# Normalising, elu parts and half of the expert scalings on ACT and POOL, and another opening, in a two-layer decoder kernel

## The reference

```python
x = _layernorm(x + _L0_attn_ref(x, ...))    # causal, 16 heads of 8; q and k normalised first
x = _layernorm(x + _L0_xattn_ref(x, ctx_1024, ctx_1024, ...))   # 16 heads, context of 154
x = _layernorm(x + _L0_ffn_ref(x, ...))     # 8 experts
x = _layernorm(x + _L1_attn_ref(x, ...))    # linear attention, phi = elu + 1
x = _layernorm(x + _L1_xattn_ref(x, ctx_1024, ...))   # 8 heads of 128, context of 154
x = _layernorm(x + _L1_ffn_ref(x, ...))     # silu(gate) * up, then down

def _layernorm(x, axis=-1, eps=1e-05):
    return (x - mean(x)) / sqrt(var(x) + eps)
# the experts
out = out + weights[:, e:e + 1] * (x @ expert_w[e] + expert_b[e])
# the linear attention
def phi(x): return jax.nn.elu(x) + 1.0
```

## Time and profile before

| | |
|---|---|
| runs | 677.26, 679.23, 681.54 us; median 679.23 |
| profiled execution | 679.57 us, span 677.8 us |
| busy | PE 526.4, DVE 443.4, ACT 294.6, POOL 144.3 us |
| granted TensorE clock, mean | 0.883 |

### The profile page before, as it was taken

One profiled execution on the slowest core, in us unless ns is written; L12 is line 12 of the kernel. 1 busy time (PEld: TensorE's weight loads), 2 busy tenths in 40 slices (PEclk: granted clock), 3 DMA queues, 4 the chain that ended last, 5 costly groups with the idle time before them and its releaser, 6 DMA issues. The chain is left out here.

```text
span 677.8 us, 12412 instructions
## 1 busy us (share of the span) xinstructions
PE 526.4 (78%) x4432; PEld 344.1 (51%) x4432; DVE 443.4 (65%) x1318; ACT 294.6 (43%) x713; POOL 144.3 (21%) x232
## 2 busy tenths in 40 slices
PE   3557798777898777887879779788897777878765
PEld 1434465433454354455755354565645464755653
DVE  3458777866788876745776988445887548456224
ACT  2333665554473243663542455753433352315631
POOL 8340002500010511222020102411202131214321
PEclk8675999977998878799978999887998989869888
DMA  7321100231200030010000000200000000000000
GB/s 197 114 82 49 49 3 24 62 87 31 55 3 2 16 81 2 16 48 2 2 18 1 3 2 10 55 2 0 18 2 1 1 1 0 1 0 16 2 0 15
DMA packets 27200, 18.19 MB, mean 27 GB/s; under 512 B 8333, under 2 KB 26885, under 8 KB 27013
## 3 DMA queue, kind: packets, MB, share of 16 engines
q1 hardware_dynamic: 22101, 13.14, 7.5%
q10 hardware_dynamic: 5040, 4.27, 2.1%
HBM read 5.58 MB, written 1.05 MB: 10 GB/s over the span
## 5 line engine op out<-in xcount | busy, mean ns | idle before, releaser
L1608 ACT ACTIVATE EX<-psum 128x1024 f32<-128x1024 f32 (+1 forms) x128 | 117.7, 975 | 54.5 <-PE psum L1209 38.7
L1809 DVE TENSOR_REDUCE nmax<-psum 128x2 f32<-128x768 f32 (+1 forms) x96 | 76.9, 862 | 20.4 <-PE psum L1182 20.1
L1176 PE MATMUL psum<-K,Q 48*128 48x154 bf16 (+4 forms) x512 | 55.9, 286 | 27.8 <-DMA K<-parts 6.9
L1804 DVE TENSOR_REDUCE nmax<-psum 128x4 f32<-128x616 f32 (+1 forms) x80 | 67.7, 876 | 8.0 <-PE psum L1176 6.5
L1203 PE MATMUL psum<-Q,K 51*128 51x512 bf16 (+3 forms) x320 | 50.2, 344 | 11.6 <-ACT EX L1608 4.2
L2073 DVE TENSOR_REDUCE nxmax<-psum 128x2 f32<-128x308 f32 x64 | 29.3, 473 | 38.3 <-PE psum L1441 37.0
L1089 POOL TENSOR_TENSOR GP<-REST,xrs 128x512 f32<-128x512 f32 (+1 forms) x48 | 32.8, 711 | 89.9 <-PE psum L1126 60.3
L1519 ACT COPY pvraw<-psum 128x512 f32<-128x512 f32 x32 | 18.7, 586 | 74.4 <-PE psum L1235 45.3
L1043 POOL TENSOR_SCALAR rstd_rest<-moments_rest 128x2 f32<-128x2 f32 x32 | 7.4, 231 | 199.5 <-DVE moments_rest L1852 199.4
L1176 PEld LDWEIGHTS psum<-K,Q 48*128 48x128 bf16 x512 | 22.0, 97 | 54.2 <-issue 31.7
L1666 ACT ACTIVATE REST<-psum,nxmax 128x154 f32<-128x154 f32 x96 | 36.1, 397 | 21.9 <-DVE nxmax L2073 14.6
(11 more groups left out here) (322 smaller groups left out, 1161.7 us busy)
## 6 DMA issues: line engine op xcount, KB each, us to landing
Q<-xparts SPq DMA_DIRECT2D x48, 64.0 KB
Q<-parts SPq DMA_DIRECT2D x42, 64.0 KB
K<-parts SPq DMA_DIRECT2D x42, 64.0 KB
X<-in_x SPq DMA_DIRECT2D x4, 256.0 KB, 2.9
Q<-in_L_xattn_Wkv ACTq DMA_DIRECT2D x1, 1024.0 KB, 7.1
Q<-mrows SPq DMA_DIRECT2D x64, 6.0 KB
K<-xkparts SPq DMA_DIRECT2D x48, 19.2 KB
out<-XB_rest SPq DMA_DIRECT2D x6, 128.0 KB, 1.9
```

The costliest lines, as they stand in the source:

```text
L1176: last = mm(to[:, r, at:at + n], Q6[a][p, b % 2, 2 * g + jj, P * q:P * q + P], K6[a][p, b % 2, 2 * g + jj, 0:n], start=True, stop=bool(a))
L1608: drains(nc.scalar.activation(dst, src, ACT.Exp), key)
L1804: last = vec.tensor_reduce(nmax[:, :, :, q], src[:, :, 0:2 * n].rearrange("p r (j k) -> p r j k", j=2), AX.X, ALU.max, negate=True)
L1809: last = vec.tensor_reduce(nmax[:, :, jj, q], src[:, :, at:at + P * (q + 1)], AX.X, ALU.max, negate=True)
```

## The change

Cost entries in `STEP_US` and a `loaded_us` table, which tells the planner when loads have landed, are new; the rule of the planner is the same. Its lists of steps differ locally.

- Every layer norm is applied by ACT as `Identity(rstd * y + shift)`; POOL computes shift = -mean * rstd, one small instruction for each block.
- The four experts of side 1 are scaled by ACT into `terms`; POOL adds the four terms with two additions; `ln` waits for them.
- ACT makes relu(x + b) and relu(-x - b); the exponential takes scale -1.
- Opening: POOL fills with ones only the half of K that batch 0 uses, then zeroes cT and eb, and the rest of `late_zeros` comes after the first root. ACT normalises k of batch 0, DVE q. Only four context transposes stand ahead of the first scores; the other ten setup steps stand among the first turns. The six weight loads stand behind ACT's placing of K.
- A few waits and semaphores are added or shared (SP's `mT` waits for the maxima placed before).

```diff
-    "ctxT": "PE .43 ACT .52", "out": "PE .85 DVE 2.2 POOL 1.4", "norm": "DVE 1.2",
+    "ctxT": "PE .43 ACT .52", "out": "PE .85 DVE 2.2 POOL 1.4", "norm": "ACT 1.4",
-    "combine": "DVE 2.3", "ln": "DVE 1.5 POOL 1.1", "lnorm": "DVE .60",
-    "x3T": "PE .22 ACT .33", "lkq": "PE .85 DVE 1.5", "phi": "ACT .55", "lv": "PE .43 DVE .35",
+    "combine": "DVE 1.5 POOL .5", "ln": "DVE 1.5 POOL 1.1", "lnorm": "ACT .73",
+    "x3T": "PE .22 ACT .33", "lkq": "PE .86 ACT 1.7", "phi": "ACT .55", "lv": "PE .43 DVE .35",
...
+def loaded_us(step):
+    b, what, *at = step
+    if what == "x0T":
+        return (4.0, 22.0, 0.0, 0.0)[b]
+    return (20.0 if at[0] < B else 50.0) if what == "wT" else 0.0
...
# SP
             def mT(b, a, g):
+                if b or g:
+                    sp.wait_ge(max_placed[a], 32 * (NQ * b + g))
...
# POOL
             for r in R:
-                nc.gpsimd.memset(words(K6[0][TILE * r + 32:TILE * r + TILE, :, :, :].rearrange(
-                    "p b h t -> p (b h) t")), TWO_ONES).then_inc(zeros_ready, 1)
+                nc.gpsimd.memset(words(K6[0][TILE * r + 32:TILE * r + TILE, 0, :, :]),
+                                 TWO_ONES).then_inc(zeros_ready, 1)
                 pool.wait_ge(zeros_ready, r + 1)
+            step(nc.gpsimd.memset(cT[:, :, :], 0.0))
+            nc.gpsimd.memset(eb[:, :, :], 0.0).then_inc(first_zeros_ready, 1)
...
+            def shifted(to, moments_, rstd_, blocks_):
+                for i in range(blocks_):
+                    last = nc.gpsimd.tensor_scalar(to[:, i:i + 1], moments_[:, i, 0:1],
+                                                   rstd_[:, i:i + 1], -1.0, ALU.mult, ALU.mult)
+                return last
...
             def rest_root(b, h, n):
                 z, of = slot(b, h), half_of(b, h)
-                pool.wait_ge(rest_stats_ready[n - 2][z], turn_in_slot(b) + 1)
-                root(of.rstd, of.moments, LN_EPS, rest_rstd_ready[n - 2][z])
+                pool.wait_ge(rest_stats_ready[z], norms_until(b, n))
+                step(root(of.rstd, of.moments, LN_EPS))
+                shifted(of.shift, of.moments, of.rstd, 2).then_inc(rest_rstd_ready[z], 1)
...
+            def add_terms(b, h, i):
+                z, of = slot(b, h), half_of(b, h)
+                k, n = place[(b, "ex", h, i, 1)]
+                pool.wait_ge(bank_drained[k], n + 1)
+                pairs = of.terms[:, i, 0:2 * D]
+                step(nc.gpsimd.tensor_tensor(pairs, pairs, of.terms[:, i, 2 * D:4 * D], ALU.add))
+                nc.gpsimd.tensor_tensor(of.X[3][:, i, :], pairs[:, 0:D], pairs[:, D:2 * D],
+                                        ALU.add).then_inc(terms_added[z], 1)
...
# ACT
             def place_first(b, r, w):
+                if w:
+                    load(late[FIRST_LATE:])
...
-                if b == 0 and n == NB - 1:
-                    load(late[FIRST_LATE:])
+            def k_norm(b):
...
+                for n in range(NB):
+                    last = nc.scalar.activation(qkn[:, n, 1, :], qkn[:, n, 1, :], ACT.Identity,
+                                                bias=qkshift[:, n:n + 1],
+                                                scale=qkrstd[:, n, 1:2])
...
+            def scaled(b, h, i):
+                z, of = slot(b, h), half_of(b, h)
+                if i == 0:
+                    act.wait_ge(gates_ready[z], turn_in_slot(b) + 1)
...
+                for e in range(4):
+                    last = nc.scalar.activation(of.terms[:, i, P * e:P * e + P],
+                                                src[:, P * e:P * e + P], ACT.Copy,
+                                                scale=of.gl[:, i, 4 + e:5 + e])
...
+            def clamp(b, h):
...
+                    nc.scalar.activation(of.lpos[:, w, :], part, ACT.Relu,
+                                         bias=col("lbk" if w else "lbq"))
+                    last = nc.scalar.activation(of.lexp[:, w, :], part, ACT.Relu,
+                                                bias=col(LESS_LB + w), scale=-1.0)
...
+            def norm(b, a, n=None):
...
+                z, of = slot(b, a), half_of(b, a)
+                act.wait_ge(rest_rstd_ready[z], norms_until(b, n))
+                dst = of.XB if n == 5 else of.X[n + 1]
+                for i in range(2):
+                    last = nc.scalar.activation(dst[:, i, :], of.Y[:, i, :], ACT.Identity,
+                                                bias=of.shift[:, i:i + 1],
+                                                scale=of.rstd[:, i:i + 1])
+                last.then_inc(rest_x_ready[z], 1)
...
# DVE: norm, clamp and side 1 of combine are gone
             def layer_norm(b, h, n):
                 if n == 2:
-                    for side in range(2):
-                        drained(dve, (b, "ex", h, 1, side))
+                    drained(dve, (b, "ex", h, 1, 0))
+                    dve.wait_ge(terms_added[slot(b, h)], 2 * turn_in_slot(b) + 2)
                     step(vec.tensor_tensor(of.Y, of.Y, of.X[3], ALU.add))
```

More of the change, by code:

```diff
@@ L471, in merged @@
             for step in group:
-                ready = max([ended[other] for other in before_it], default=0.0)
+                ready = max([ended[other] for other in before_it],
+                            default=loaded_us(group[0]))
                 if step[1] in REST_STEPS and step[1] != "x2T":
@@ L623, in build @@
         qkrstd = sb("qkrstd", [P, NB, 2])
+        qkshift = sb("qkshift", [P, NB])
+        shift = [sb("shift_attn", [P, NB]), sb("shift_rest", [P, 2 * NB])]
         wqkv_p = sb("wqkv_p", [P, 3 * D])
@@ L743, in build @@
             of.kp, of.AT = within(scratch, 6 * HS, 2, D), within(scratch, 7 * HS, 2, P)
+            of.terms = within(scratch, 0, 2, 4 * D)
             of.XPT, of.XPR = within(scratch, 0, XH, P), within(scratch, XH * P, 2, P)
@@ L795, in build @@
         gates_ready = [sem(f"gates_ready{z}") for z in range(4)]
+        terms_added = [sem(f"terms_added{z}") for z in range(4)]
         phi_exps = [sem(f"phi_exps{z}") for z in range(4)]
@@ L1652, in phi_ @@
                 lexp = half_of(b, h).lexp
-                nc.scalar.activation(flat(lexp), flat(lexp), ACT.Exp
+                nc.scalar.activation(flat(lexp), flat(lexp), ACT.Exp, scale=-1.0
                                      ).then_inc(phi_exps[slot(b, h)], 1)
@@ L1691, in hidden @@
                                      ).then_inc(htanh_ready[slot(b, h)], 1)
+            def norm(b, a, n=None):
+                if n is None:
+                    act.wait_ge(rstd_ready[a], b + 1)
+                    if a == 0 and b:
+                        filled(act, (b - 1, "x1T", 1))
+                        act.wait_ge(residual_ready, b)
+                    if a and turn_in_slot(b):
+                        for h in HALVES:
+                            drained(act, (b - 1, "mb", h))
+                    for i in range(NB):
+                        dst = half_of(b, i // 2).X[2][:, i % 2, :] if a else X1[:, i, :]
+                        last = nc.scalar.activation(dst, Y_attn[:, i, :], ACT.Identity,
+                                                    bias=shift[0][:, i:i + 1],
+                                                    scale=rstd[0][:, i:i + 1])
+                    last.then_inc(x_ready[a + 1], 1)
+                    return
+                z, of = slot(b, a), half_of(b, a)
[6 more added lines that the diff above has]
+                last.then_inc(rest_x_ready[z], 1)
             def half_T(b, h, n):
                 move(half_of(b, h).xT[n], (b, f"x{n}T", h), HS)
-            work = {"qkv": qkv, "qkT": qkT, "place": place_first,
+            work = {"qkv": qkv, "qk_norm": k_norm, "qkT": qkT, "place": place_first,
                     "xk": lambda b: cross_split(b, 1), "xq": lambda b: cross_split(b, 0),
@@ L2118, in cross_weights @@
                 vec.tensor_scalar(col(XBQ), col("xbq"), HEAD_SCALE, None, ALU.mult)
+                for w in range(2):
+                    vec.tensor_scalar(col(LESS_LB + w), col("lbk" if w else "lbq"), -1.0, None,
+                                      ALU.mult)
                 for r in R:
```

151 lines of the change are left out of this document (72 added, 79 removed).

## The result

| | us | against before |
|---|---|---|
| before | 678.5 (677.3 to 681.5) | |
| after | 701.3 (698.9 to 704.5) | 1.033 [1.027, 1.039] |
| forecast | 671.0 (656 to 688) | |

The change makes the kernel 3.3% slower; the forecast said 1.1% faster. In the profiled executions the span grows from 677.8 to 700.9 us. PE's busy time grows from 526.4 to 539.4 and the rest of its span from 151.4 to 161.5. So 10 of the 23 us are gaps, and 13 are the same 4432 products taking longer: the granted clock is 0.863 in place of 0.883.

A forecast was written before the change was run, and what follows sets the result against it. PE was taken as nearest to the bound, with what can be won in its gaps. From 679.6 us: opening −5.8, DVE's relief −9.2, middle norms +3, ACT's load +2, tail +1.4, giving 671.0; 8-in-10 range 656 to 688.

The forecast's parts named there:

- Term 1: Opening: first score product 8.4 us earlier, at 36.15, less setup moved behind the first scores; 5.8 us less in all.
- so 2.6 stays: Opening: of 6.2 us of late setup on PE, 3.6 is paid by shorter waits on DVE, leaving 2.6.
- Term 2: Middle stretch (236 to 530 us): DVE relieved, its share 69% to 56%, so PE waits less on it; 9.2 us less.
- The line drawn through three stretches: PE's non-norm waits on DVE interpolated from DVE's share; at 56% it gives 8.5 us in place of 17.7.
- Term 3: Norms in the middle grow by 0.7 per pair and 1.3 per four blocks, partly hidden by DVE's lateness; 3 us more.
- Term 4: ACT takes on about 75 us of work; PE's waits on it are hand-overs that do not grow with load; 2 us more.
- Term 5: Tail: one norm wait goes, 3.5 less; the other six and the last norm grow, 4.9 more; 1.4 us more in sum.
- the 3.5 that were to go: Tail: the 3.54 us wait before the transposes at 576.00 vanishes through a new order and fewer scalings on DVE.
- The third: Rival: ACT stands at norms for POOL's shift with exponentials behind, at most 33 us; 692 us, above 686; chance 0.14.
- a plan that packs the turns differently from the small local moves: Planner's order: named as something that would make the forecast wrong, with no size or chance given.
- The clock: Granted clock: a difference of more than 0.02 was named as something that would make the forecast wrong.
- rival 1: Middle: DVE set the pace far more than PE's direct waits show; 657.5 us, range 650 to 664; chance 0.21.

The follow-up runs named there:

- e1: Kernel before with only the new opening; norms, clamps and expert scalings stay on DVE and are counted there: 677.1 us, 1.001 of before.
- e16: e1 with only the 32 clamps moved to ACT, e1's order held: 675.3 us, 0.996 of before.
- e15: e1 with clamps on ACT and half of the expert scalings on ACT and POOL, e1's order held: 684.1 us, 1.010 of before.
- e5: e1 with normalising of x on ACT and POOL's shift, planner costs and order untouched: 699.6 us, 1.030 of before.
- e6: e1 with only the planner's norm and lnorm costs changed to ACT's, all work on DVE: 697.5 us, 1.030 of before.
- e3: e1 with after's planner costs and order, norms, clamps and scalings still on DVE: 695.7 us, 1.035 of before.
- e2: After with e1's four cost entries, so all work moved in e1's order: 702.0 us, 1.049 of before.
- e14: e1 with POOL also computing the shift and DVE, still normalising, waiting for it; e1's order: 688.2 us, 1.015 of before.
- e13: e5 without POOL's shift instructions (mean not subtracted), norms on ACT in e1's order: 694.6 us, 1.026 of before.
- e18: Kernel before, own opening and order, with only the clamps on ACT (and after's shared semaphores): 673.0 us, 0.999 of before.
- e7: e1 with only the planner's combine and lkq costs changed to after's, all work on DVE: 690.8 us, 1.019 of before.
- e8: Control: e1 with the planner's time between engines at 0.22 in place of 0.2, no work moved: 697.1 us, 1.028 of before.
- e11: Control: e1 with the planner's time between engines at 0.18 in place of 0.2, no work moved: 685.2 us, 1.011 of before.
- e17: The same kernel as e16 (e1 with clamps on ACT), run again with more rounds: 678.4 us, 1.012 of before.

## Why the prediction was wrong

**Term 1** (opening, 5.8 less). The path up to the first score product held: 36.91 for 36.15, the bank's copy of qkn as releaser. The closeness is in part luck: the normalising on DVE took 3.79 us, not 2.4, beside POOL's fill, and ACT's placing ended at 31.0 for 29.4, but the six loads then held ACT for 5.0 us and not 5.95. What failed is "so 2.6 stays": of 7.7 us of lead 2.2 to 3.0 are left one turn later, because PE now waits 4.07 us for maxima and has the setup still to do, and by itself the opening brings nothing that e1 could show.

**Term 2** (DVE's relief, 9.2 less) is the step that failed. DVE did become free, if by 46 us and not 66: it worked 397.0 us for 375 forecast and 443.4 before (by e16, e15 and e5 the clamps took 11.4 off it, the scalings 9.8, the norms 26.3; the largest error is the scalings, 64 at 0.28 in the forecast). PE's waits on DVE in the middle other than norms went from 17.7 to 16.1, not to 8.5. The line drawn through three stretches left two things out. The first is the order: waits on DVE depend on where the planner puts PE's step behind DVE's. e6 and e3 show it, in which DVE's work is that of e1 and PE's waits for mparts go from 11.4 to 18.7 and 20.0. The second is where the work went. With e1's order held (e2) the relief does lower these waits, from 17.7 to 11.9 at a DVE share of 57%, two thirds of what the line promised; but in the same stretch PE's waits on POOL grow from 4.8 to 9.5, for norms from 8.5 to 13.3 and on ACT otherwise from 18.8 to 21.1. So 5.8 us came back and 11.8 were added.

**Term 3** (norms in the middle, 3 more) has the right sign there, 8.1 to 10.0, and nearly the size. But e3, with DVE's norms in the same order, has 17.4 in that stretch, so the agreement is no test of the term. And its reason, that DVE's lateness covers the shift, is refuted by e14: 6.4 us of waits and 11.0 us of time over the run. The sizes: shift 0.267 apiece where I took at most 0.231; on ACT 0.88 for a pair of blocks where I took 0.78 (twice 0.39). The estimate from the Trainium skill (ScalarE: Activation LUTs, "What ACT_TABLE_LOAD costs"), 0.48 alone and 0.39 for one that overlaps, fits: one instruction lasts 0.487 in the mean, two in a row 0.86 to 0.90, four 1.65. I had used the second figure for the first of each row as well, which is small. The Trainium skill's rule to keep such work on VectorE ("Rules for kernel authors"), which I set aside for the equal prices of single instructions, points the right way for the norms (e13: 17.4 us), but the page's reason is a price per element, and e16 to e18 show no loss from relu on ACT, which the same rule names.

**Term 4** (ACT's load, 2 more) failed too. "They are hand-overs and do not grow with its load": PE's waits on ACT other than norms grew from 18.6 to 25.9 in the middle, 7.3 more for the 2 of the term (over the three stretches from 41.6 to 47.3; with the norms, 78.2).

**Term 5** (tail, 1.4 more). PE's waits for norms there went from 11.9 to 16.5, 4.6 more for 4.9 forecast, but the 3.5 that were to go did not: in place of the 3.54 us of the earlier trace rows stand 2.88 us at 599.43, now behind eight exponentials on ACT. The stretch from the last PV to the end grew by 10.6, at a clock of 0.81 in place of 0.87.

**The rivals.** The third, slower by ACT standing at the norm, was nearest: 692, with 31 us of standing of the 33 I had as its most, and PE's waits for norms at 30.9 of the 35 I had set as its mark. e2, e5, e13 and e14 show that mechanism in e1's order. That its marks were met in after is in part luck: e3 meets that of the waits (29.9) without it, and after is 5.6 us above e3. So it is not the whole: "a plan that packs the turns differently from the small local moves" stood among what would make me wrong, without a price or a chance. It costs as much as the mechanism does (e3, e6, e7, e8, e11: 8 to 20 us), with no work moved at all. Which of the two one calls the cause of the 23 us depends on the path: from e1, the order first costs 18.6 and the moves then 5.6; the moves first cost 24.9 and the order then nothing. I read the difference of the orders as small and local; it was the largest risk of the change.

**The clock.** It differed by 0.020, which I had named as the bound. The loss of after is 13 us of PE's busy time and 10 of gaps, and the sum had no term for the first. In the table above PE's busy time for the same products is 515.6 at 0.901 and 539.4 at 0.863. Kernels with more gaps tend to have the lower clock, but only loosely (e14 has 159.6 us of gaps at 0.886, e8 156.6 at 0.868), and ten executions of e1 alone go from 0.875 to 0.903, so whether the gaps drive it is not shown.

**The working.** Three slips in it change no conclusion: 443.4 less 66 is 377, not 375; the chance of a time over 686 stands as 0.14 and as 0.15; and two thirds of the forecast's band added to rival 1 give 0.49, not 0.51.

**What stays open:** why e1's and before's orders are so much better, and why the clock falls with the others. e8 has no new large wait; it loses by many small ones and by leaving more work to the end. That before's order was found by search is a guess.

## What to carry to other kernels

Where a planner writes the order, a change of engine costs is two changes; time each alone, with a control that disturbs the order for no reason. A relief of the engine next to the bound earns only what lies behind a wait that ends there last, less what waits behind the same work on its new engine; a line through stretches says neither. An operation whose operands are made by one engine more has its chain lengthened in every place at once: count that chain per place where PE waits, and take it as showing in full unless a row shows what covers it.

## What the runs showed of the hardware

Four 128x128 normalisings on DVE took 3.79 us beside POOL's fill of K (15.62 to 19.31), 0.95 apiece, where the later ones of this size took 0.32 apiece (11.5 us over 36); ACT's four in the same window took 1.65. Before, eight took 4.80. That the fill is the cause was not tested.

One kernel, profiled twice, e16 and then e17:

```profile
core 0: 667.5 us, clock 0.898
```

```profile
core 0: 676.5 us, clock 0.884
```

The same instructions differ by 9.0 us, 7.5 of them in PE's busy time (520.0 and 527.5). Over these sets of runs before itself took from 666 to 687 us. Effects below some 5 us need many runs here, whatever the trace of a single one says.
